# GpSimd subtracts the softmax maxima of all sixteen attention units of a block, not of eight

## The chip, the core and the metric

One core of one Trainium2 chip. The metric is the device time of one execution in microseconds; the time before is the median of three executions. The profile comes from one more execution.

## What is computed

A decoder layer over 64 sequences of 128 tokens with 128 features: self-attention with 16 heads and relative positions, cross-attention, a mixture of experts, each followed by a layer norm. The change touches the first part alone:

```python
scores = jnp.einsum('bhqd,bhkd->bhqk', q, k) / scale
scores = scores + (c2p + p2c) / scale            # relative positions
probs = jax.nn.softmax(scores, axis=-1)
ctx = jnp.einsum('bhqk,bhkd->bhqd', probs, v)
out = ctx @ Wo + bo + hidden_states
mu = jnp.mean(out, axis=-1, keepdims=True)
var = jnp.mean(jnp.square(out - mu), axis=-1, keepdims=True)
out = (out - mu) * jax.lax.rsqrt(var + LN_EPS) * ln_scale + ln_bias
x = _layernorm(x + out)
```

## The kernel before

The attention stage works on 16 blocks of four sequences. A block has sixteen **units**; a unit `u` is one sequence and four heads, so four score matrices of 128 x 128. Each engine has its own program, a loop over the steps `u` of a block, and the order of an engine's work is the order in which this code is written. Semaphores tie the engines together.

What happens to one unit: TensorE writes the scores to a PSUM bank (L448, L451; two banks). VectorE adds the second position term and takes the row minimum (the scores are negated), which leaves `T` and `nm` in SBUF (L709, four times a main instruction and a read of the accumulator; it raises `t_ok`). ScalarE makes `E`, the exponential. TensorE transposes `E` two steps later (L459), ScalarE copies the transposed tile to `ET` three steps later (L601), and TensorE multiplies by the values (L485) four steps later. `T` and `E` have three buffers each, chosen by `u % 3`.

The exponential has two forms. In units of `EARLY_MAX`, 6 to 13, GpSimd first subtracts the minimum in place (L369, `take_max`, which waits for `t_ok` and raises `p_ok`), and ScalarE runs one instruction of 128 x 512 (L610). In the other units, 0 to 5, 14 and 15, GpSimd isn't asked; ScalarE runs four of 128 x 128, each with its head's minimum as its bias (L613).

Between these steps stands other work. Steps 0 to 2: the next block's inputs are transposed and projected (TensorE L402, L407, L408, L412; ScalarE L574 and L582; VectorE L676 and L683). From step 6 on, 16 bucket tiles of the next block, two in a step: TensorE L425, ScalarE L588 (`HM`), VectorE L693. After step 15 come the next block's position chunks (TensorE L440, copied out by ScalarE L596 and VectorE L702), while the last units are finished; here ScalarE's L620 copies the sums of four units to `OC`, and that frees the bank for the next L485.

The two layer norms of the block before are spread over the steps of this one by `NORM_STEPS`: on VectorE statistics at step 2 (L731), variances at 3 (L738, L741), `centred` at 4 (L751), `first_norm` at 5 (L759), the second norm's statistics and variances at 6 and 7 (L731, L738, L741), its end at 9 (L766). The inverse roots are powers on GpSimd (L365, `power`): it waits for VectorE's L741, and L759 and L766 wait for it.

GpSimd does its work of a block in this order: `copy_block` (L299, `XB` for the next block), the first power, units 6 and 7, the second power, units 8 to 13, `residuals` (L304 twice), `spread_keys` (L313, then L315 four times, which makes `KD` for the next block's scores), `values_out` (L323).

Of the kernel before, what the change touches and what calls it, by code (L numbers as in the profile page):

```python
# [39 lines left out]
NORM_STEPS = (2, 3, 4, 5, 6, 7, 9)  # L40
# [1 line left out]
CONSTS, TAB, BUILT = 21, 10, 4  # L42
DVE_CHUNKS = tuple((c, 1) for c in range(1, CHUNKS))
ACT_CHUNKS = tuple((c, f) for c in range(CHUNKS) for f in range(2) if (c, f) not in DVE_CHUNKS)
EARLY_MAX = range(6, 14)
VCOLS = 32
HALVES = ((0, 0), (0, 1), (1, 0))

# [94 lines left out]
def attention_stage(nc, held, dr, X):  # L143

    with ExitStack() as ctx:
# [6 lines left out]
        def sem(name):  # L152
            return held.enter_context(nc.semaphore("a_" + name))
# [74 lines left out]
        t_ok = Count(sem("t_ok"), UNITS, credit=2)  # L228
        p_ok = Count(sem("p_ok"), len(EARLY_MAX))
        e_ok = Count(sem("e_ok"), UNITS, credit=3)  # L230
# [63 lines left out]
        def _(pool):  # L294
            def copy_block(i, nxt):
                if nxt:
                    hold(pool, spare_pool, xT_ps.sem, xT_ps.at(i, 1))
                at = (i + 1) * NB if nxt else 0
                pool.tensor_copy(XB[:, :, :], X[:, bass.ds(at, NB), :]).then_inc(xb.sem, 1)  # L299

            def residuals(i):
                hold(pool, spare_pool, link_s.sem, link_s.at(i, 0))
                for vec, dst in ((bo_all, XO), (bias_all, XL)):
                    pool.tensor_tensor(dst[:, :, :], X[:, bass.ds(i * NB, NB), :],  # L304
                                       vec[:, :].rearrange("p (a h) -> p a h", a=1).to_broadcast([P, NB, H]),
                                       ALU.add).then_inc(x_ok.sem, 1)

            def spread_keys(i, nxt):
                if nxt:
                    hold(pool, spare_pool, s_ps.sem, s_ps.at(i, UNITS))  # L310
                hold(pool, spare_pool, qn_in.sem, qn_in.at(i, qn_in.per * (1 + nxt)))
                hold(pool, spare_pool, kn_in.sem, kn_in.at(i, kn_in.per * (1 + nxt)))
                pool.tensor_copy(QS[:, :, :, :], QN[:, :, :, :].rearrange("p g s b -> p g b s"))  # L313
                for h in range(HG):
                    last = pool.tensor_scalar(KD[:, :, h, :, :], KN[:, :, :, :].rearrange("p g s b -> p g b s"),  # L315
                                              group_mask[:, h:h + 1], 1.0, ALU.mult, ALU.mult)
                last.then_inc(kd_ok.sem, 1)

            def values_out(i, nxt):
                if nxt:  # L320
                    hold(pool, spare_pool, pv.sem, pv.at(i, UNITS))
                hold(pool, spare_pool, vn_ok.sem, vn_ok.at(i, 1 + nxt))
                pool.tensor_copy(V[:, :, :, 0:DH], VN[:, :, :, :]).then_inc(v_ok.sem, 1)  # L323
# [39 lines left out]
            def power(i, n):  # L363
                pool.wait_ge(var_ok.sem, var_ok.at(i, n + 1))
                pool.tensor_tensor(rstd[:, :], rstd[:, :], half[:, :], ALU.pow).then_inc(rstd_ok.sem, 1)  # L365

            def take_max(i, u):
                hold(pool, spare_pool, t_ok.sem, t_ok.at(i, u + 1))
                pool.tensor_tensor(T[:, u % 3, :, :], T[:, u % 3, :, :],  # L369
                                   nm[:, u % 3, :].rearrange("p (h a) -> p h a", a=1).to_broadcast([P, HG, S]),  # L370
                                   ALU.subtract).then_inc(p_ok.sem, 1)

            def body(i, first=False, last=False):
                if not last:
                    copy_block(i, 1)
                if not first:
                    power(i - 1, 0)
                for u in range(UNITS):
                    if u in EARLY_MAX:
                        take_max(i, u)  # L380
                    if u == NORM_STEPS[5] and not first:
                        power(i - 1, 1)
                residuals(i)
                if not last:
                    spread_keys(i, 1)
                    values_out(i, 1)

            body(0, first=True)
            with pool.Fori(1, NBLK - 1) as i:
                body(i)  # L390
            body(NBLK - 1, last=True)
            for n in range(2):
                power(NBLK - 1, n)
# [177 lines left out]
        def _(act):  # L571
# [31 lines left out]
            def exponentials(i, u):  # L603
                if u in EARLY_MAX:
                    act.wait_ge(p_ok.sem, p_ok.at(i, EARLY_MAX.index(u) + 1))
                else:
                    act.wait_ge(t_ok.sem, t_ok.at(i, u + 1))
                act.wait_ge(et_ps.sem, et_ps.at(i, u - 2))
                if u in EARLY_MAX:
                    act.activation(E[:, u % 3, :, :], T[:, u % 3, :, :], ACT.Exp, scale=-1.0).then_inc(e_ok.sem, 1)  # L610
                    return
                for h in range(HG):
                    last = act.activation(E[:, u % 3, h, :], T[:, u % 3, h, :], ACT.Exp, bias=nm[:, u % 3, h:h + 1],  # L613
                                          scale=-1.0)
                last.then_inc(e_ok.sem, 1)
# [1535 lines left out]
```

## Time and profile before

| what | value |
|---|---|
| three executions | 2919.28, 2921.62, 2922.58 us; median 2921.62 us |
| the profiled execution | 2919.2 us; its span in the profile is 2917.4 us |
| busy over the span | PE 2411.7, DVE 2223.2, ACT 2293.1, POOL 711.4 us |
| blocks' loop of the attention stage | about 73 to 1030 us |

Times within the span are counted from its start. PE is TensorE, DVE VectorE, ACT ScalarE, POOL GpSimd. In a timeline a row gives the start, the length and the instruction; "x4" is four instructions in a row, and brackets say how long the engine stood idle before and who released it. In a group by line the number before the bar is the sum and the mean length in ns (the lengths overlap, since an engine starts the next instruction before the last one has ended); behind the bar stands the idle time before these instructions.

### The profile page before, as it was taken

The page shows a single profiled execution, that of the slowest core. Times are in us where ns is not written, and L with a number is a line of the kernel's source. Part 1 is how long each engine was busy: PE and PEld are TensorE (multiplying, and loading weights), DVE is VectorE, ACT ScalarE, POOL GpSimd, SP SyncE. Part 2 cuts the span into 40 slices and gives each one's busy share as a digit, 9 for nine tenths or more (in the row PEclk, how much of TensorE's full clock was granted, in tenths as well). Part 3 has the DMA queues.
Part 4 walks back from the last instruction along what each step waited for, and adds up shares of the span by engine and source line. Part 5 has one row for each costly group of instructions (what it writes and reads, how often), then busy time and mean ns, then how long its engine had stood idle before and what let it go on. Part 6 is the DMA issues. An engine that isn't in the chain of part 4 may idle for free. (4 is left out here: it accounts for less than half of the span.)

```text
span 2917.4 us, 64307 instructions
## 1 busy us (share of the span) xinstructions
PE 2411.7 (83%) x18180; PEld 1323.8 (45%) x18199; DVE 2223.2 (76%) x6591; ACT 2293.1 (79%) x4255; POOL 711.4 (24%) x565
## 2 busy tenths in 40 slices
PE   2777777777777724865779999999999999999997
PEld 1555555555555413642434444444444444444443
DVE  3677777777777667777558888888888888888887
ACT  1777777777777635333679999999999999999996
POOL 3334353344334400122411111111111111111114
PEclk7899999999999956988789999999999999999999
DMA  3000000000000010000011121121111211111113
GB/s 76 13 17 17 11 11 12 20 11 11 11 17 15 1 42 1 0 29 0 0 36 53 43 58 43 44 58 43 53 49 43 58 43 45 56 43 56 45 43 87
DMA packets 182540, 96.04 MB, mean 33 GB/s; under 512 B 22539, under 2 KB 179291, under 8 KB 182491
## 3 DMA queue, kind: packets, MB, share of 16 engines
q1 hardware_dynamic: 182491, 95.45, 11.7%
q8 instruction: 23, 0.38, 0.1%
q14 instruction: 26, 0.21, 0.0%
HBM read 78.10 MB, written 4.73 MB: 28 GB/s over the span
## 5 line engine op out<-in xcount | busy, mean ns | idle before, releaser
L1971 DVE TENSOR_TENSOR c_Hl<-c_HF,c_Hh 128x512 f16<-128x512 f32 x1028 | 679.6, 688 | 161.2 <-ACT c_Hh L1858 144.9
L1854 ACT ACTIVATE c_HF<-c_H,c_b 128x512 f32<-128x512 f32 x1028 | 710.6, 691 | 64.4 <-PE c_H L1793 44.4
L1858 ACT ACTIVATE c_Hh<-c_H,c_b 128x512 f16<-128x512 f32 x1028 | 706.1, 687 | 0.0
L1909 POOL TENSOR_TENSOR c_EX<-c_euler,c_D 128x16 f32<-128x16 f32 x65 | 188.6, 2902 | 1195.2 <-DVE c_D L1944 1195.2
L1791 PE MATMUL c_H<-c_Ch,SH 128*128 128x512 f16 x1028 | 390.7, 380 | 0.0
L1792 PE MATMUL c_H<-c_Cl,SH 128*128 128x512 f16 x1028 | 390.6, 380 | 0.0
L1793 PE MATMUL c_H<-c_Ch,SH 128*128 128x512 f16 x1028 | 390.5, 380 | 0.0
L1802 PE MATMUL c_Y<-c_Hh,SH 128*128 128x512 f16 x1024 | 388.1, 379 | 0.1
L1804 PE MATMUL c_Y<-c_Hl,SH 128*128 128x512 f16 x1024 | 388.1, 379 | 0.0
L1803 PE MATMUL c_Y<-c_Hh,SH 128*128 128x512 f16 x1024 | 388.1, 379 | 0.0
L709 DVE CUSTOM_DVE_ANT_0 a_T<-a_S,a_POS 128x128 f32<-128x128 f32 x1024 | 234.9, 285 | 70.0 <-PE a_S L451 63.1
L459 PE MATMUL a_E<-a_ident,a_E 128*128 128x128 f32 x1024 | 159.5, 279 | 67.5 <-ACT a_ET L601 66.8
L693 DVE TENSOR_TENSOR a_AB<-a_G,a_HM 128x512 f16<-128x512 f32 x256 | 164.4, 683 | 65.2 <-ACT a_HM L588 61.6
L588 ACT ACTIVATE a_HM<-a_G,a_low_rows 128x512 f16<-128x512 f32 x256 | 161.9, 686 | 63.1 <-PE a_G L425 63.1
L369 POOL TENSOR_TENSOR a_T<-a_T,a_nm 128x512 f32<-128x512 f32 x128 | 133.3, 1041 | 300.2 <-DVE a_nm L709 300.2
L613 ACT ACTIVATE a_E<-a_T,a_nm 128x128 f32<-128x128 f32 x512 | 162.8, 390 | 54.5 <-DVE a_nm L709 53.0
L1979 DVE SCALAR_TENSOR_TENSOR c_PR<-c_Y,c_b,c_CWB 128x512 f32<-128x512 f32 x256 | 191.1, 747 | 2.4 <-DMA c_CWB<-c_rows 1.5
L485 PE MATMUL a_O<-a_ET,a_V 128*32 128x128 f32 x2048 | 110.4, 288 | 66.6 <-ACT a_OC L620 66.6
L451 PE MATMUL a_S<-a_ident,a_POS 128*128 128x128 f32 x1024 | 160.8, 280 | 0.0
L1793 PEld LDWEIGHTS c_H<-c_Ch,SH 128*128 128x128 f16 x1028 | 100.7, 98 | 122.2 <-issue 1.4
L1802 PEld LDWEIGHTS c_Y<-c_Hh,SH 128*128 128x128 f16 x1024 | 100.1, 98 | 121.8 <-issue 0.6
L1804 PEld LDWEIGHTS c_Y<-c_Hl,SH 128*128 128x128 f16 x1024 | 100.2, 98 | 120.8
(296 smaller groups left out, 4382.7 us busy)
## 6 DMA issues: line engine op xcount, KB each, us to landing
c_CWB<-c_rows SPq DMA_DIRECT2D x260, 256.0 KB, 4.1
a_QN<-a_QH SPq DMA_DIRECT2D x128, 32.0 KB, 1.8
a_KN<-a_KH SPq DMA_DIRECT2D x128, 32.0 KB, 1.8
out<-d_O SPq DMA_DIRECT2D x16, 256.0 KB, 2.3
a_QN<-a_QL SPq DMA_DIRECT2D x64, 32.0 KB, 1.9
a_KN<-a_KL SPq DMA_DIRECT2D x64, 32.0 KB, 1.8
CUR<-in_ctx SPq DMA_DIRECT2D x1, 1848.0 KB
c_rows<-c_CWR SPq DMA_DIRECT2D x65, 8.0 KB, 1.4
```

What stands on the lines that cost most here:

```text
L709: last = dve.tensor_tensor_reduce(out=T[:, u % 3, h, :], in0=bS[u % 2][:, h * S:(h + 1) * S], in1=POS[:, h // 2, row_x(1, g, h % 2, b), :] ...
L1791: pe.matmul(dst, W1h[:, e, cols], Ch[:, j, :], start=True, stop=False)
L1792: pe.matmul(dst, W1h[:, e, cols], Cl[:, j, :], start=False, stop=False)
L1793: pe.matmul(dst, W1l[:, e, cols], Ch[:, j, :], start=False, stop=True).then_inc(h_ps.sem, 1)
L1802: pe.matmul(dst, W2h[:, e, f, :], Hh[:, g % 2, f, :], start=f == 0, stop=False)
L1803: pe.matmul(dst, W2l[:, e, f, :], Hh[:, g % 2, f, :], start=False, stop=False)
L1804: last = pe.matmul(dst, W2h[:, e, f, :], Hl[:, g % 2, f, :], start=False, stop=f == OC - 1)
L1854: act.activation(HF[:, k % 4, :], bH[k % 4][:, :], ACT.Gelu_apprx_tanh, bias=b1[:, g % EXPERTS, f:f + 1], scale=1.0 / WSCALE).then_inc(hf_ ...
L1858: act.activation(Hh[:, g % 2, f, :], bH[k % 4][:, :], ACT.Gelu_apprx_tanh, bias=b1[:, g % EXPERTS, f:f + 1], scale=1.0 / WSCALE).then_inc( ...
L1909: pool.tensor_tensor(EX[:, :, :].rearrange("p t e -> p (t e)"), euler[:, :], D[:, :, :].rearrange("p t e -> p (t e)"), ALU.pow).then_inc(e ...
L1971: dve.tensor_tensor(Hl[:, g % 2, f, :], HF[:, k % 4, :], Hh[:, g % 2, f, :], ALU.subtract)\
L1979: dve.scalar_tensor_tensor(PR[:, g % 2, :], bY[g % 2][:, :], b2[:, e:e + 1], CWB[:, m, e, :], ALU.add, ALU.mult).then_inc(p_ok.sem, 1)
```

## The change

`EARLY_MAX` covers all sixteen units, so `take_max` is called sixteen times in a block, and ScalarE takes the one-instruction form everywhere. The first power moves from ahead of the units to behind the subtraction of unit 3 (`NORM_STEPS[1]`); the second stays where it was, behind that of unit 7 (`NORM_STEPS[5]`).

```diff
-EARLY_MAX = range(6, 14)
+EARLY_MAX = range(0, 16)
...
                 if not last:
                     copy_block(i, 1)
-                if not first:
-                    power(i - 1, 0)
                 for u in range(UNITS):
                     if u in EARLY_MAX:
                         take_max(i, u)
-                    if u == NORM_STEPS[5] and not first:
-                        power(i - 1, 1)
+                    if u in (NORM_STEPS[1], NORM_STEPS[5]) and not first:
+                        power(i - 1, (NORM_STEPS[1], NORM_STEPS[5]).index(u))
                 residuals(i)
```

GpSimd's program of the last block, where the rows stand unrolled (`a_rstd` is written by a power, `a_T` by `take_max`, `a_XO` and `a_XL` by `residuals`):

```order
-L365 TENSOR_TENSOR a_rstd<-a_rstd,a_half 128x4
-L369 TENSOR_TENSOR a_T<-a_T,a_nm 128x512 x2
-L365 TENSOR_TENSOR a_rstd<-a_rstd,a_half 128x4
-L369 TENSOR_TENSOR a_T<-a_T,a_nm 128x512 x6
...
+L369 TENSOR_TENSOR a_T<-a_T,a_nm 128x512 x4
+L365 TENSOR_TENSOR a_rstd<-a_rstd,a_half 128x4
+L369 TENSOR_TENSOR a_T<-a_T,a_nm 128x512 x4
+L365 TENSOR_TENSOR a_rstd<-a_rstd,a_half 128x4
+L369 TENSOR_TENSOR a_T<-a_T,a_nm 128x512 x8
 L304 TENSOR_TENSOR a_XO<-X,a_bo_all 128x512
 L304 TENSOR_TENSOR a_XL<-X,a_bias_all 128x512
```

Six subtractions now stand ahead of unit 6's, four of them ahead of the first power, and two more stand ahead of the residuals, which in the other blocks have `spread_keys` behind them.

ScalarE's program at steps 3 to 6 of a block, before the change:

```order
L601 ACTIVATE a_ET<-a_E 128x512
L613 ACTIVATE a_E<-a_T,a_nm 128x128 x4
L601 ACTIVATE a_ET<-a_E 128x512
L613 ACTIVATE a_E<-a_T,a_nm 128x128 x4
L601 ACTIVATE a_ET<-a_E 128x512
L588 ACTIVATE a_HM<-a_G,a_low_rows 128x512 x2
L610 ACTIVATE a_E<-a_T 128x512
```

The same steps after the change (two lines shorter, so 601 is 599, 610 is 608 and 588 is 586):

```order
L599 ACTIVATE a_ET<-a_E 128x512
L608 ACTIVATE a_E<-a_T 128x512
L599 ACTIVATE a_ET<-a_E 128x512
L608 ACTIVATE a_E<-a_T 128x512
L599 ACTIVATE a_ET<-a_E 128x512
L586 ACTIVATE a_HM<-a_G,a_low_rows 128x512 x2
L608 ACTIVATE a_E<-a_T 128x512
```

The order is the same; four narrow instructions have become one wide one, and the exponential still stands ahead of the copy `ET` and the tiles `HM`.

## Rows read from the trace of the kernel before

**Rows 1.** Group by line, attention stage: the narrow exponentials.

```profile
L613 ACT ACTIVATE a_E<-a_T,a_nm 128x128 f32<-128x128 f32 x512 | 162.8, 390 | 54.5 <-DVE a_nm L709 53.0
```

**Rows 2.** Stretches of one block: length, then each engine's busy time, TensorE's clock.

```profile
510.16:518.56 8.40, 7.35 (x71) 5.23 (x69) 8.18 (x54) 7.01 (x20) 1.53 (x2) 1.00 0.19 51
562.00:564.00 2.00, 2.00 (x11) 1.74 (x10) 0.93 (x8) 0.63 (x1) 0.00 (x0) 0.50 0.00 0
```

**Rows 3.** Timeline of ScalarE, units 3 to 7 of that block.

```profile
512.49 1.28 ACT L613 ACTIVATE a_E<-a_T,a_nm 128x128 f32<-128x128 f32 x4 [1.28 <-DVE a_nm L709]
...
516.00 1.28 ACT L613 ACTIVATE a_E<-a_T,a_nm 128x128 f32<-128x128 f32 x4
...
517.67 1.25 ACT L588 ACTIVATE a_HM<-a_G,a_low_rows 128x512 f16<-128x512 f32 x2
...
521.93 0.63 ACT L610 ACTIVATE a_E<-a_T 128x512 f32<-128x512 f32 x1 [0.54 <-POOL a_T L369]
522.47 0.58 ACT L620 ACTIVATE a_OC<-a_O 128x512 f32<-128x512 f32 x1
```

**Rows 4.** Timeline of VectorE, units 3 to 7 of that block, some rows.

```profile
512.78 0.17 DVE L741 TENSOR_SCALAR a_rstd<-a_mv 128x4 f32<-128x4 f32 x1
...
513.99 1.13 DVE L751 SCALAR_TENSOR_TENSOR a_R<-a_R,a_mv,a_scale_all 128x128 f32<-128x128 f32 x4
...
515.89 1.14 DVE L759 SCALAR_TENSOR_TENSOR a_R<-a_R,a_rstd,a_XL 128x128 f32<-128x128 f32 x4
...
518.56 1.27 DVE L693 TENSOR_TENSOR a_AB<-a_G,a_HM 128x512 f16<-128x512 f32 x2
...
520.59 0.09 DVE L709 DVE_READ_ACCUMULATOR2_ANT a_nm<- 128x1 f32 x1
...
521.00 0.92 DVE L741 TENSOR_SCALAR a_rstd<-a_mv 128x4 f32<-128x4 f32 x1
```

**Rows 5.** Timeline of GpSimd, unit 7.

```profile
520.86 1.04 POOL L369 TENSOR_TENSOR a_T<-a_T,a_nm 128x512 f32<-128x512 f32 x1 [1.77 <-DVE a_nm L709]
```

**Rows 6.** All instructions of three lines: shortest, median and longest in ns.

```profile
L741 DVE TENSOR_SCALAR a_rstd<-a_mv x32: 170/172/922, 157.1 to 1026.4; 128x4 f32<-128x4 f32 x32
...
L2084 DVE SCALAR_TENSOR_TENSOR d_nb<-d_mv,d_rstd x16: 147/150/547, 2883.3 to 2912.6; 128x4 f32<-128x4 f32 x16
...
L1321 POOL COPY b_r<-SH x64: 392/399/994, 1149.3 to 1269.9; 77x256 f32 x64
```

**Rows 7.** Timelines, VectorE beside GpSimd: the output stage, then the last block.

```profile
2887.88 0.55 DVE L2084 SCALAR_TENSOR_TENSOR d_nb<-d_mv,d_rstd 128x4 f32<-128x4 f32 x1 [1.06 <-POOL d_rstd L2051]
...
2887.80 0.61 POOL L2043 COPY d_CB<-CUR 128x512 f32 x1
...
1022.46 1.13 DVE L751 SCALAR_TENSOR_TENSOR a_R<-a_R,a_mv,a_scale_all 128x128 f32<-128x128 f32 x4
...
1022.63 1.05 POOL L365 TENSOR_TENSOR a_rstd<-a_rstd,a_half 128x4 f32<-128x4 f32 x1 [13.47 <-DVE a_rstd L741]
```

**Rows 8.** Timelines at the block's unit 15: ScalarE, then VectorE.

```profile
545.22 1.28 ACT L613 ACTIVATE a_E<-a_T,a_nm 128x128 f32<-128x128 f32 x4 [0.87 <-DVE a_nm L709]
546.41 0.57 ACT L620 ACTIVATE a_OC<-a_O 128x512 f32<-128x512 f32 x1
...
548.08 0.69 DVE L702 COPY a_POS<-a_S 128x512 f32<-128x512 f32 x1 [2.89 <-PE a_S L440]
```

**Rows 9.** Timelines, GpSimd's ends of three blocks, and the next block's first scores.

```profile
482.20 1.27 POOL L304 TENSOR_TENSOR a_XO<-X,a_bo_all 128x512 f32<-128x512 f32 x1
...
540.72 1.28 POOL L304 TENSOR_TENSOR a_XO<-X,a_bo_all 128x512 f32<-128x512 f32 x1
...
546.40 8.51 POOL L315 TENSOR_SCALAR a_KD<-a_KN,a_group_mask 128x2048 f16<-128x2048 f16 x4
...
601.11 1.27 POOL L304 TENSOR_TENSOR a_XO<-X,a_bo_all 128x512 f32<-128x512 f32 x1
...
561.15 0.47 PE L448 MATMUL a_S<-a_KD,a_QS 96*128 96x512 f16 x1 [1.12 <-DVE a_POS L702]
```

## The prediction

> **What bounds the kernel now.** I read the busy shares first: TensorE, VectorE and ScalarE are all between 76 and 83%, GpSimd is at 24%, so no single engine is full. The attention stage is then a matter of who waits for whom, step by step, and the views that count are the timelines of one block.
>
> In the groups by line, look at what ended the idle time ahead of the narrow exponentials: 53.0 of 54.5 us ended with VectorE's L709, and their instructions are 162.8 us of busy time [rows 1]. A narrow exponential starts as soon as VectorE has released it in about half of the units. For those units the latency from L709 to `E` counts, and not how long ScalarE is busy.
>
> From the copy of the values at 510.16 to the first `HM` tile's use at 518.56, VectorE is busy 8.18 of 8.40 us [rows 2]. It is the bound of steps 3 to 5, where the first layer norm is squeezed in, while ScalarE has 1.4 us to spare. At unit 5 ScalarE starts at 516.00, 0.11 us behind the start of L759, which itself follows unit 5's L709 on VectorE [rows 3, 4]. So ScalarE keeps pace with VectorE there and hasn't a queue to work off. The next thing, two `HM` tiles at 517.67, stands on ScalarE behind unit 5's exponential and one `ET` copy; VectorE's L693 at 518.56 needs the first of them, and had about 0.2 us to spare (half of 1.25 us after 517.67 is 518.3) [rows 3, 4].
>
> At the end of a block the chain is plainer: unit 15's exponential at 545.22 waited 0.87 us for VectorE; `OC` follows at 546.41; it frees the bank for the product L485, behind which the position chunks stand on TensorE, and VectorE, with nothing to do, waits 2.89 us until the first chunk reaches it at 548.08 [rows 8].
>
> **The change, part by part.**
>
> *The hop through GpSimd.* Unit 7 shows it: the last accumulator read ends at 520.68, the subtraction runs from 520.86 to 521.90, the wide exponential starts at 521.93 [rows 3 to 5]. That is 1.25 us after L709, against some 0.05 us for a narrow one: 1.2 us more.
>
> *The exponential.* From the start of a narrow one to the next instruction pass 1.19 us (545.22 to 546.41), from the start of a wide one 0.54 us (521.93 to 522.47) [rows 3, 8]. It gives back 0.65 us, eight times a block. Where ScalarE was waiting for VectorE, what stands behind the exponential is therefore 1.2 - 0.65 = 0.55 us later. The gain could only count where ScalarE was late already, in unit 1 for instance; but there the projections on TensorE and then VectorE set the pace, so I cost it at nothing.
>
> *Collision with L741.* The variance add L741 takes 170 to 172 ns in half of its 32 cases and up to 922 ns [rows 6]. The long one of the block read here, at 521.00, lies in unit 7, right behind L709: the subtraction of unit 7 runs until 521.90 and L741 ends at 521.92 [rows 4, 5]. The one in unit 3, at 512.78, is short, since GpSimd has nothing to do there [rows 4]. After the change unit 3 looks like unit 7: the subtraction is asked for at the same distance from L709, so this L741 takes 0.92 us too. That is 0.75 us on VectorE, in the stretch where VectorE is the bound, in 15 blocks.
>
> *Collision with `centred` and `first_norm`.* L751 and L759 (1.13 and 1.14 us for four) read two tensors from SBUF [rows 4]. No row of before has one of them beside a subtraction, so the price is bounded. Below: beside a power L751 kept its 1.13 us (1022.46, power at 1022.63), so nothing [rows 7]; but the power reads four elements a partition and the subtraction 512. Above: L2084, also with two tensors in SBUF, takes 150 ns and once 547; there a GpSimd copy of 512 elements ran from 2887.80 to 2888.41, and L2084 ended at 2888.43 [rows 6, 7]. So it was held until the copy had ended. The subtraction is nearer to this copy, and I take a full hold. Who loses? GpSimd's copy L1321, 399 ns as a rule, took 994 ns once, so GpSimd can be the one who is held [rows 6]. In the block, with VectorE 0.75 us late, `centred` runs from 514.74 to 515.87 and the subtraction of unit 4 is asked for at 515.0: it waits 0.87 us and runs to 516.91. `first_norm` wants to start at 516.64. If it goes first at 516.91, the subtraction of unit 5 runs from 518.05 to 519.09, the exponential starts at 519.12, an `ET` copy follows at 519.66 and `HM` at 520.14, 2.5 us later than 517.67. If the subtraction of unit 5 goes first, to 517.95, `first_norm` and all of VectorE behind it are 2.1 us late instead. Less the 0.2 us that L693 had to spare: L693 is 1.9 to 2.3 us late, and I take 2.1. Without these two holds it would be 0.75 + 0.55 - 0.2 = 1.1 us. The Trainium skill, SBUF — State Buffer, section "Who interferes with whom", says that a VectorE instruction with two SBUF inputs contends with a GpSimd instruction that reads SBUF, and that the one that comes second is blocked wholly. By that rule the block loses the 2.1 us, and L2084's row agrees; L751 beside the power doesn't show such a block.
>
> From unit 6 on all three engines and GpSimd are late by about the same, and their program isn't changed, so nothing there gives it back. The second L741 and L766 already stand beside a subtraction.
>
> *Units 14 and 15.* The exponential of 14 has slack before TensorE uses it. Unit 15's delay goes to `OC`, the product, the chunks and VectorE's 2.89 us wait: 0.55 us [rows 8].
>
> *GpSimd's end of the block.* The residuals started at 540.72, before unit 15 was done; now they start when its subtraction ends, 545.2 + 0.18 + 1.04 = 546.4 [rows 8, 9]. Two residuals (2.5 us), L313 (2.0) and L315 (8.51) bring `KD` to 559.4; the next scores, which need it, started at 561.15 and will start 0.55 us later [rows 9]. Margin 2.3 us, so this costs nothing; `XB`, 1.2 us behind `KD`, is wanted 0.65 us behind the start of the scores and has 1.7 us. The transfers of queries and keys wait for older `KD`, and don't move.
>
> *The sum.* 15 blocks with a norm (2.1 + 0.55) = 39.8 us; block 0, without a norm, 0.9 us (0.55 at its end, some 0.3 ahead of the tiles). Together 40.7 us on the profiled execution's 2919.2: 2959.9 us. That execution was 2.4 us below the median of 2921.62, so the forecast is **2962 us**.
>
> **The rivals.**
>
> *Only L741 collides* (L751 and L759 pass untouched, as beside the power): 15 x (1.1 + 0.55) + 0.9 = 25.7 us, 2947 us. For it: L751's row. Against it: L2084's.
>
> *Faster: the hop is hidden.* `T` and `E` have three buffers, so the hop may vanish and ScalarE's saving count. 65 of the 128 narrow exponentials weren't waiting for VectorE (it ended the idle time in 63 cases); they would give 65 x 0.65 = 42 us at most, the 63 others cost 63 x 0.55 = 35: 7 us faster, 2915 us. It decides only if ScalarE had a queue to work off in steps 3 to 5. Against it: ScalarE had 1.4 us free there and VectorE 0.2 [rows 2], and the collisions come on top.
>
> *GpSimd's chain becomes the bound.* If `KD` needs 3 us more than worked out, each of 15 blocks loses 0.7 us more: 2973 us. It decides from 2.3 us on. Against it: L315's durations hardly vary.
>
> *The clock.* Some blocks take longer: from 482.20 to 540.72 are 58.52 us, to 601.11 are 60.39 [rows 9]. In the second TensorE stood idle around 561 and the granted clock fell to 0.50, its lower level, from 562 to 564 [rows 2]. Six of 14 such intervals are long. A shifted rhythm can give this to more blocks or fewer: 8 x 1.9 = 15 us more (2977) or 11 us less (2951). Longer idle times speak for more.
>
> *No change:* the delays would have to be swallowed by VectorE's waits in units 8 to 13; nothing there is early while the rest is late.
>
> **How the numbers follow.** Two full holds 50%, only L741 20%, more through clock or GpSimd 15%, hidden hop and faster 8%, within 0.2% (about what a measurement of this kernel tells from no change, 6 us) 7%. The range runs from the L741 case less a few clock dips, 2943, to the two holds with all dips and a late `KD`, 2986. Faster 0.08, same 0.07, slower 0.85.
>
> **What would show it.** The L741 of unit 3 at 0.92 us in 15 blocks; L751 or L759 lengthened, or some subtractions of 1.9 us; the exponential of unit 15 1.2 us behind L709, VectorE's wait for the first chunk at 3.4 us; `KD` ready before the next scores, which still wait for VectorE; about 61 us for a block that took 58.5. I am wrong if blocks stay at 58.5 us, if L741 of unit 3 stays at 0.17 us, or if the scores at a block's start wait for GpSimd.

## The result, and the profile after

The changed kernel takes 2966.16 us (median of four executions, 2959.89 to 2970.15) against 2921.85 us for the kernel before: a ratio of 1.0148, 95% interval 1.0134 to 1.0162. It is 44 us slower. The profiled execution has a span of 2968.4 us and a mean granted clock of 0.933; the one of before had 2917.4 us and 0.941.

In the changed kernel's code the lines behind the change stand two lower: L741, L751, L759, L693, L709 are now L739, L749, L757, L691, L707, and the only exponential left is L608.

First the timeline of VectorE in the changed kernel, steps 2 to 6 of one middle block (start, length, instruction):

```profile
474.98 0.69 DVE L681 TENSOR_TENSOR a_VN<-a_M,a_bv_all 128x512 f32<-128x512 f32 x1 [0.59 <-PE a_M L410]
...
477.61 0.92 DVE L739 TENSOR_SCALAR a_rstd<-a_mv 128x4 f32<-128x4 f32 x1
479.28 1.92 DVE L749 SCALAR_TENSOR_TENSOR a_R<-a_R,a_mv,a_scale_all 128x128 f32<-128x128 f32 x4
481.96 1.97 DVE L757 SCALAR_TENSOR_TENSOR a_R<-a_R,a_rstd,a_XL 128x128 f32<-128x128 f32 x4
484.70 0.86 DVE L729 BATCH_NORM_STATS2 a_st<-a_R 128x6 f32<-128x128 f32 x4
485.48 1.27 DVE L691 TENSOR_TENSOR a_AB<-a_G,a_HM 128x512 f16<-128x512 f32 x2
```

And GpSimd beside it, the subtractions of units 3, 4 and 5 with the first power between:

```profile
477.46 1.04 POOL L369 TENSOR_TENSOR a_T<-a_T,a_nm 128x512 f32<-128x512 f32 x1 [1.85 <-DVE a_nm L707]
478.60 1.02 POOL L365 TENSOR_TENSOR a_rstd<-a_rstd,a_half 128x4 f32<-128x4 f32 x1
479.60 1.19 POOL L369 TENSOR_TENSOR a_T<-a_T,a_nm 128x512 f32<-128x512 f32 x1
482.22 1.04 POOL L369 TENSOR_TENSOR a_T<-a_T,a_nm 128x512 f32<-128x512 f32 x1 [1.43 <-DVE a_nm L707]
```

All three VectorE steps of the first norm have grown: the variance add from 0.17 to 0.92 us, `centred` from 1.13 to 1.92, `first_norm` from 1.14 to 1.97 [rows 4]. Together that is 2.37 us. The subtraction of unit 4 started 0.32 us behind `centred` and took 1.19 us where the others take 1.04: it lost 0.15 us and then held VectorE. `first_norm` was overtaken 0.26 us after its start, and there the subtraction lost nothing (1.04 us). L691 follows the statistics at once: VectorE, and nothing else, is late there. The moved power ends at 479.62, and `first_norm`, which needs it, follows VectorE's L707 at 481.96 without a wait. The stretch from the copy of the values to the first tile was 8.40 us long (510.16 to 518.56) and is 10.50 us now (474.98 to 485.48).

All instructions of these lines: shortest, median, longest in ns. With 32 variance adds a median of 919 says that more than half are long, as against 172 before [rows 6]; of the 64 instructions of each norm step only one in four is held, and then for some 0.8 us.

```profile
L739 DVE TENSOR_SCALAR a_rstd<-a_mv x32: 170/919/921, 162.6 to 1076.9; 128x4 f32<-128x4 f32 x32
...
L749 DVE SCALAR_TENSOR_TENSOR a_R<-a_R,a_mv,a_scale_all x64: 335/341/1127, 164.3 to 1073.7; 128x128 f32<-128x128 f32 x64
...
L757 DVE SCALAR_TENSOR_TENSOR a_R<-a_R,a_rstd,a_XL x64: 339/342/1184, 167.0 to 1075.0; 128x128 f32<-128x128 f32 x64
```

At unit 15, timelines of ScalarE and, a block earlier, of VectorE and GpSimd:

```profile
514.07 0.63 ACT L608 ACTIVATE a_E<-a_T 128x512 f32<-128x512 f32 x1 [2.25 <-POOL a_T L369]
514.61 0.58 ACT L618 ACTIVATE a_OC<-a_O 128x512 f32<-128x512 f32 x1
...
454.38 0.69 DVE L700 COPY a_POS<-a_S 128x512 f32<-128x512 f32 x1 [3.46 <-PE a_S L438]
...
452.10 1.26 POOL L304 TENSOR_TENSOR a_XO<-X,a_bo_all 128x512 f32<-128x512 f32 x1
...
456.55 8.51 POOL L315 TENSOR_SCALAR a_KD<-a_KN,a_group_mask 128x2048 f16<-128x2048 f16 x4
...
467.46 0.39 PE L446 MATMUL a_S<-a_KD,a_QS 96*128 96x512 f16 x1 [1.12 <-DVE a_POS L700]
```

VectorE's wait for the first chunk has gone from 2.89 to 3.46 us [rows 8]. `KD` is ready at 465.06, 2.4 us before the next block's first scores at 467.46, which wait for VectorE as before [rows 9].

To see where a block's time goes I cut it at three points of VectorE's timeline, each from start to start: **head**, from the copy of the values to the first tile (L693); **middle**, from there to the first copy of a position chunk out of bank S (L702); **tail**, from there to the next block's copy of the values. Among the 14 intervals of each kernel these values recur to 0.01 us in the shortest ones (six intervals before, two after):

```
               head   middle   tail    sum
before         8.42   29.51    20.60   58.53
after         10.50   30.07    20.60   61.17
difference     2.08    0.56     0       2.64
```

The head is 10.50 in thirteen of the fourteen intervals after, and 8.42 (or 8.40, 8.41) in twelve before. The one of the fourteen that isn't longer, 8.52 in both kernels, is that of block 0, which has no norm. Middle and tail are longer in some blocks of either kernel, and there the granted clock is lower; in five intervals of the changed kernel a middle of 30.7 us or more is followed by a tail of 20.41. The stretches below are of the changed kernel (length; busy time of TensorE, of its weight load, of VectorE, ScalarE and GpSimd; the clock; the DMA share and rate): a block and a bit with 0.84, and within it 18 us at the lower level, 0.50; the interval ahead of the head shown above, from 413.30, had 0.97.

```profile
413.30:475.00 61.70, 46.71 (x590) 31.63 (x589) 46.63 (x202) 41.15 (x76) 32.82 (x28) 0.97 0.05 13
327.00:345.00 18.00, 15.97 (x271) 12.04 (x268) 11.57 (x27) 10.44 (x21) 10.49 (x8) 0.50 0.00 0
284.00:350.00 66.00, 52.39 (x590) 35.78 (x591) 47.30 (x205) 41.63 (x76) 32.72 (x27) 0.84 0.04 12
```

The 14 intervals sum to 831.6 us before and 874.5 after, 42.9 more. Thirteen of them have a norm in the head and one, block 0's, has none: 13 x 2.64 + 0.56 = 34.9. The other 8 us stand in intervals whose clock is lower, 4.7 of them in block 0's (60.0 us before at a clock of 0.97, 65.3 after at 0.84). The profiled spans differ by 51 us: 37.0 in the 14 blocks with a norm and tiles, 0.6 for the hop in block 0, 8 of slower clock, 4.7 in the last block, and 0.7 ahead of the first interval and behind the attention stage.

### The profile page after: what moved, and what is told of

It reads as the page before. It is cut to its first block and busy times, and to the rows that moved or that the text cites. A ratio compares the mean times of both kernels' runs of the same rounds, so it can differ in the third digit from the quotient of the medians.

```text
span 2968.4 us, 64207 instructions
## 1 busy us (share of the span) xinstructions
PE 2441.2 (82%) x18180; PEld 1336.7 (45%) x18199; DVE 2259.3 (76%) x6591; ACT 2211.8 (75%) x3871; POOL 844.6 (28%) x693
## 5 line engine op out<-in xcount | busy, mean ns | idle before, releaser
L369 POOL TENSOR_TENSOR a_T<-a_T,a_nm 128x512 f32<-128x512 f32 x256 | 268.3, 1048 | 476.6 <-DVE a_nm L707 476.1
L608 ACT ACTIVATE a_E<-a_T 128x512 f32<-128x512 f32 x256 | 161.4, 630 | 229.3 <-POOL a_T L369 228.4
L707 DVE CUSTOM_DVE_ANT_0 a_T<-a_S,a_POS 128x128 f32<-128x128 f32 x1024 | 234.5, 284 | 68.3 <-PE a_S L449 59.3
L457 PE MATMUL a_E<-a_ident,a_E 128*128 128x128 f32 x1024 | 166.6, 288 | 87.8 <-ACT a_ET L599 86.3
L691 DVE TENSOR_TENSOR a_AB<-a_G,a_HM 128x512 f16<-128x512 f32 x256 | 164.3, 683 | 63.6 <-ACT a_HM L586 58.9
L457 PEld LDWEIGHTS a_E<-a_ident,a_E 128*128 128x128 f32 x1024 | 120.7, 147 | 109.6 <-ACT a_E L608 93.1
```

What stands on the lines that cost most here:

```text
L369: pool.tensor_tensor(T[:, u % 3, :, :], T[:, u % 3, :, :], nm[:, u % 3, :].rearrange("p (h a) -> p h a", a=1).to_broadcast([P, HG, S]), AL ...
L457: last = pe.transpose(bE[slot_of(w) % 2][:, h * S:(h + 1) * S], E[:, w % 3, h, :], ident[:, :])
L707: last = dve.tensor_tensor_reduce(out=T[:, u % 3, h, :], in0=bS[u % 2][:, h * S:(h + 1) * S], in1=POS[:, h // 2, row_x(1, g, h % 2, b), :] ...
```

## The experiments

Each kernel is compared with the kernel before on the same chip; the line numbers of the rows are those of each kernel. All that differ in `EARLY_MAX` alone keep the power in its new place.

**Units 14 and 15 alone.**

```diff
-EARLY_MAX = range(0, 16)
+EARLY_MAX = range(6, 16)
```

> GpSimd subtracts in units 6 to 15 (8 to 13 of before, and the two last), units 0 to 5 keep four narrow exponentials. My theory has two separate places per block: the hop in unit 15 costs 0.55 us in each of 16 blocks and the rest of the loss lies in units 3 to 5. It expects about 9 us over the kernel before (some 2931 us), the wait of VectorE for the first chunk at 3.4 to 3.5 us and the variance add of step 3 at 0.17 us. A rival, that GpSimd's late end of the block (keys for the next one) costs as well, expects more, 15 to 25 us, with the first scores waiting for GpSimd.

2932.48 us against 2921.55, ratio 1.0045 (1.0028 to 1.0062). The wait has its 3.46 us, here in VectorE's timeline:

```profile
496.65 0.69 DVE L700 COPY a_POS<-a_S 128x512 f32<-128x512 f32 x1 [3.46 <-PE a_S L438]
```

Head 8.42, middle 30.08, tail 20.60. Eleven microseconds of 44, where 9 were expected. The rival of a late `KD` falls: the shortest blocks lose 0.57 us and nothing in the tail, and the next block's first scores still wait for VectorE (L700, 1.12 us).

**Units 0 to 5 alone.**

```diff
-EARLY_MAX = range(0, 16)
+EARLY_MAX = range(0, 14)
```

> GpSimd subtracts in units 0 to 13, units 14 and 15 keep four narrow exponentials. My theory expects 2.1 us in each of the 15 blocks with a norm, about 32 us over before (some 2954 us), with the variance add of step 3 at 0.92 us and both four-instruction norm steps at about 1.95 us. If the two places weren't additive, this run and the one with units 14 and 15 alone would not add up to the 44 us of the whole change.

2955.41 us, ratio 1.0113 (1.0096 to 1.0130): 34 us. Head 10.50, middle 29.49 where undisturbed. 11 + 34 is 45, so the two places add up to the whole change (44).

**Units 0, 1, 2.**

```diff
-EARLY_MAX = range(0, 16)
+EARLY_MAX = (0, 1, 2) + tuple(range(6, 14))
```

> GpSimd subtracts in units 0, 1, 2 and 6 to 13. There the hop is present but no VectorE instruction of the kinds that were held stands behind it. If the loss in the first half comes from the holds, this is within 3 us of before. If the hop through GpSimd itself costs 0.55 us each time that ScalarE waited for VectorE (unit 2 did), it is up to 8 us slower.

2921.79 us, ratio 0.9998 (0.9988 to 1.0007); head 8.42. The hop is there in three more units and costs nothing, and neither does the power's new place.

**Unit 3.**

```diff
-EARLY_MAX = range(0, 16)
+EARLY_MAX = (3,) + tuple(range(6, 14))
```

> GpSimd subtracts in unit 3 and 6 to 13. Only the variance add L741 of step 3 can be held: 0.75 us in 15 blocks, 11 us over before (2933 us). If a hold on VectorE there were absorbed, it is as before; if the hop were what costs, it adds 0.55 us a block to it, about 19 us.

2934.55 us, ratio 1.0046 (1.0029 to 1.0062): 13 us. The variance add is held here too, and the two norm steps aren't (longest instruction 347 and 351 ns). But the 0.75 us of the hold become 0.48 in the head, 8.89 to 8.90 us, and in five blocks the head is 10.04, so that the 11 us expected were nearly met by luck. The timeline of VectorE in such a block, and the two stretches, long and short:

```profile
456.23 0.93 DVE L739 TENSOR_SCALAR a_rstd<-a_mv 128x4 f32<-128x4 f32 x1
...
463.64 1.29 DVE L691 TENSOR_TENSOR a_AB<-a_G,a_HM 128x512 f16<-128x512 f32 x2 [0.56 <-ACT a_HM L586]
...
453.60:463.64 10.04, 8.40 (x69) 5.88 (x68) 9.05 (x54) 6.38 (x17) 3.10 (x3) 0.83 0.19 52
635.01:643.90 8.89, 7.25 (x71) 5.23 (x69) 8.86 (x54) 6.38 (x17) 2.58 (x3) 1.00 0.19 52
```

With the clock at 0.83 in this stretch instead of 1.00, L691 waits for ScalarE's tile. The clock stood at 0.50 from 459 to 462, behind a wait of TensorE of 1.64 us that the short heads have as well, so why it fell in these five is open. In all 14 intervals of the kernel before the head stayed within 8.40 to 8.59. Fifteen heads at 0.48 us more are 7.2 us and the five long ones add 5 x 1.15 = 5.8, together the 13.

**Units 4 and 5.**

```diff
-EARLY_MAX = range(0, 16)
+EARLY_MAX = (4, 5) + tuple(range(6, 14))
```

> GpSimd subtracts in units 4, 5 and 6 to 13; unit 3 keeps its narrow exponentials. Only the two norm steps with two SBUF inputs can be held, 0.79 and 0.83 us by the changed kernel's profile. The head run lost 2.08 us in its shortest blocks and the unit-3 run 0.48, so 1.6 us a block, 24 us over before (about 2945 us), with both steps at about 1.95 us for four and the variance add of step 3 at 0.17. If the holds only occur because unit 3's hold has shifted VectorE against GpSimd, both steps stay at 1.13 us and the run is as before.

2952.99 us, ratio 1.0106 (1.0088 to 1.0124): 31 us, 7 more than expected. The head is 10.11, that is 1.70 us more, close to the 1.6 that I expected; but no block has both middle and tail at their shortest, with a mean clock of 0.934 over the run. So both norm steps are held without unit 3's help: their longest instructions take 1197 and 1183 ns where the kernel before has 351 and 352, 1.68 us together. All subtractions take 1.04 us here, so that GpSimd loses nothing. That is VectorE's timeline of a block, the variance add short and `centred` long:

```profile
465.21 0.17 DVE L739 TENSOR_SCALAR a_rstd<-a_mv 128x4 f32<-128x4 f32 x1
...
466.42 1.99 DVE L749 SCALAR_TENSOR_TENSOR a_R<-a_R,a_mv,a_scale_all 128x128 f32<-128x128 f32 x4
```

**Steps that read one tensor from SBUF.** In both kernels `centred` and `first_norm` become statistics of the same rows; what they compute is left out.

```diff
-                    last = dve.scalar_tensor_tensor(R[:, b, :], R[:, b, :], mv[:, b, 0:1], scale_all[:, :],
-                                                    ALU.subtract, ALU.mult)
+                    last = dve.bn_stats(st[:, b, :], R[:, b, :])
...
-                    last = dve.scalar_tensor_tensor(R[:, b, :], R[:, b, :], rstd[:, b:b + 1], XL[:, b, :],
-                                                    ALU.mult, ALU.add)
+                    last = dve.bn_stats(st[:, b, :], R[:, b, :])
```

> The kernel before with both norm steps (centred and first_norm) replaced by statistics of the same rows, which read one SBUF tensor; it leaves out the centring and the first normalisation. Four statistics take 0.87 us, four of the steps 1.13, so up to 0.5 us a block less: 2913 to 2922 us. It is the base for the next one.

> The changed kernel with the same two steps replaced by statistics (centring and first normalisation left out). If a second SBUF input is what exposes a VectorE instruction to GpSimd's subtraction, the statistics keep 0.87 us and this is only 16 to 26 us slower than its base (variance add and the hop of unit 15). If the loss in units 4 and 5 is the hop through GpSimd or any VectorE instruction is held, it is 40 to 45 us slower than its base, as in the unaltered pair.

2920.63 us for the first (ratio to the kernel before 0.9993, 0.9975 to 1.0010) and 2955.23 for the second (1.0111, 1.0093 to 1.0129). On the first question the trace of the second is plain. In its list of instructions the statistics beside the subtractions take what they take elsewhere:

```profile
L749 DVE BATCH_NORM_STATS2 a_st<-a_R x64: 269/272/287, 164.0 to 1060.9; 128x6 f32<-128x128 f32 x64
```

Of the 128 statistics in the place of the two steps 105 overlap a subtraction, so these steps aren't held, and the rival that any VectorE instruction is held falls. That the second SBUF tensor is what exposes the norm steps isn't shown by it alone: the statistics also write 6 columns instead of 128, and the variance add, which is held, reads one tensor. The time is 35 us above its base, where I had expected 16 to 26. The head went from 8.09 to 9.10 us, the middle from 29.53 to 30.10, so 1.58 us in the shortest block, 24 us in 15; the rest goes with a slower clock (mean 0.929; 13 of the 14 intervals are longer than the shortest). And 1.0 us in the head is more than one held variance add: L691 waits 0.50 us for ScalarE's tile there.

**The variance add as another instruction.** The eps stands as a third column beside mean and variance, and a reduction over two columns gives the same sum. First in the kernel before:

```diff
-        mv = sb("mv", [P, NB, 2])
+        mv = sb("mv", [P, 2, NB, 3])
...
-                dve.tensor_scalar(rstd[:, :], mv[:, :, 1], (1e-7, 1e-5)[k], None, ALU.add).then_inc(var_ok.sem, 1)
+                dve.tensor_reduce(rstd[:, :], mv[:, k, :, 1:3], AX_X, ALU.add).then_inc(var_ok.sem, 1)
```

> The kernel before with the variance add made as a tensor_reduce over the variance and a constant beside it, the same sum. If the kind of instruction decides, none of its 32 cases lasts 0.92 us any more, where 15 did. If VectorE is the bound in step 7, that gives 0.75 us in 15 blocks, 11 us (2911 us); if the wait for the tiles behind it takes it up, the time is within 3 us of before. If every instruction with an SBUF input were held, the 0.92 us stay.

2923.41 us, ratio 1.0005 (0.9995 to 1.0015). All 32 take 160 to 165 ns in its trace, 15 of them beside a subtraction, and the shortest blocks keep 58.53 us. The kind of instruction decides, and in step 7 of the kernel before the hold of 0.75 us cost nothing. Then in the changed kernel:

> The changed kernel with the variance add as a tensor_reduce, the same sum. No variance add is held any more. With the two norm steps still held, I expect what unit 3 alone cost to come back: 0.5 to 0.75 us in 15 blocks, 8 to 11 us less than the changed kernel's 2966, so 2955 to 2958. If the subtraction of unit 3 then only meets the next VectorE instructions and costs the same there, it stays at 2966.

2958.24 us, 8 us less than the changed kernel (ratio to the kernel before 1.0125, 1.0108 to 1.0142, as against 1.0148). Timeline of VectorE:

```profile
465.87 0.16 DVE L741 TENSOR_REDUCE a_rstd<-a_mv 128x4 f32<-128x8 f32 x1
467.08 1.92 DVE L751 SCALAR_TENSOR_TENSOR a_R<-a_R,a_mv,a_scale_all 128x128 f32<-128x128 f32 x4
```

The head is 10.04 instead of 10.50, so removing unit 3's hold gives back 0.46 us, as much as adding it alone had cost (0.48).

**Unit 14.**

```diff
-EARLY_MAX = range(0, 16)
+EARLY_MAX = range(6, 15)
```

> GpSimd subtracts in units 6 to 14. My theory says that the exponential of unit 14 has slack before TensorE uses it, and that unit 15 alone costs the 0.58 us of the tail: the time is that of before within 3 us and the wait of VectorE for the first chunk stays at 2.89 us. If both units share the loss, it is about 5 us slower and the wait about 3.2 us.

2922.10 us, ratio 0.9995 (0.9984 to 1.0005); the wait is 2.89 us again:

```profile
494.67 0.69 DVE L700 COPY a_POS<-a_S 128x512 f32<-128x512 f32 x1 [2.89 <-PE a_S L438]
```

The loss at the end of a block is unit 15's alone.

**All units where nothing was to pay.**

```diff
-EARLY_MAX = range(0, 16)
+EARLY_MAX = (0, 1, 2) + tuple(range(6, 15))
```

> GpSimd subtracts in units 0, 1, 2 and 6 to 14: all those where I found nothing to pay. ScalarE is relieved of 4 x 0.65 us a block. If ScalarE's saving were worth anything where it is free, this would be faster than before; my theory says no change, within 3 us.

2922.81 us, ratio 1.0008 (0.9998 to 1.0019). Relieving ScalarE of 2.6 us a block in these four units is worth nothing. No experiment pointed to a version faster than the kernel before.

**Nothing that can be held.** The changed kernel with the reduction and with both norm steps replaced by statistics.

> The changed kernel without any VectorE instruction that can be held in steps 3 to 5: the variance add as a reduce, the two norm steps replaced by statistics (centring and first normalisation left out). What is left against its base (the kernel before with the same replacement, shortest blocks 58.22 us) is the hop: 0.57 us at unit 15 and, if the hop also reaches the tiles behind unit 5, 0.55 us there, so shortest blocks of 59.3 us and 17 us more in all. If the hop is hidden in steps 3 to 5, blocks of 58.8 us and 9 us more.

2963.81 us (2952.50 to 2970.10), ratio to the kernel before 1.0146 (1.0115 to 1.0177). This expectation failed: I had said 17 us above the base of 2920.63, and it is 43. The head is 8.96; the shortest middle is 30.10 and the undisturbed tail 20.59, though no block has both: 59.65 together, 1.43 us above the base's 58.22, of which 0.87 in the head, where I had allowed 0.55. That is 21 us in 15 blocks. The other half goes with the clock: the profiled execution's mean of 0.924 is the lowest of all the profiled ones, and the four executions of this kernel go from 2952.50 us at 0.928 to 2970.10 us at 0.917. Stretches of its trace, two middles that should be 30.1 us long and one head:

```profile
408.70:440.80 32.10, 23.46 (x222) 15.05 (x221) 20.61 (x101) 21.72 (x41) 13.24 (x14) 0.92 0.03 8
471.00:502.00 31.00, 22.31 (x206) 14.36 (x204) 19.82 (x100) 20.62 (x39) 12.80 (x13) 0.92 0.03 7
399.70:408.70 9.00, 7.31 (x69) 5.03 (x68) 7.83 (x54) 5.27 (x10) 5.70 (x6) 1.00 0.19 52
```

In the head nothing is held any more, and its last part shows what bounds it: ScalarE's tiles wait for TensorE's L425, behind the exponentials that came late.

```profile
405.29 0.63 ACT L610 ACTIVATE a_E<-a_T 128x512 f32<-128x512 f32 x1 [0.87 <-POOL a_T L371]
...
407.89 1.27 ACT L588 ACTIVATE a_HM<-a_G,a_low_rows 128x512 f16<-128x512 f32 x2 [0.24 <-PE a_G L425]
...
408.70 1.29 DVE L693 TENSOR_TENSOR a_AB<-a_G,a_HM 128x512 f16<-128x512 f32 x2 [0.35 <-ACT a_HM L588]
```

So the hop does cost in the head when it is alone, and VectorE waits for ScalarE there. It isn't added to the holds. In the changed kernel ScalarE begins its two tiles at 484.30, so that the first is done at about 484.9, and VectorE comes to it at 485.48:

```profile
484.30 1.26 ACT L586 ACTIVATE a_HM<-a_G,a_low_rows 128x512 f16<-128x512 f32 x2
```

Of two delays on parallel ways the longer counts. The 0.87 us are measured against a head that the replacement had shortened to 8.09 us; against the 8.42 of the kernel before they are 0.54, so they can't be carried over to the norm steps as they were.

## Why the prediction was right

*The size and the sign.* 2962 us forecast, 2966 measured, within the range; the likeliest case came. A block was to lose 2.1 + 0.55 us and loses 2.08 + 0.56 in the shortest ones. That the 2.1 came out to 0.02 us is luck in part, as the third paragraph shows.

*"Collision with L741": the hold was right, its price wasn't.* It is held in all 15 blocks for 0.75 us as forecast. Alone it moved the head by 0.48. The timelines show where the rest went: before, VectorE's next instruction started 0.19 us behind the end of L741 (512.95 to 513.14), and now it starts 0.09 us ahead of that end (478.44, 478.53). That takes up 0.28 of the 0.75 us. The two rows, of the kernel before and of the changed one:

```profile
513.14 0.29 DVE L709 CUSTOM_DVE_ANT_0 a_T<-a_S,a_POS 128x128 f32<-128x128 f32 x1 [0.19 <-issue]
```

```profile
478.44 0.28 DVE L707 CUSTOM_DVE_ANT_0 a_T<-a_S,a_POS 128x128 f32<-128x128 f32 x1
```

*"Collision with `centred` and `first_norm`": the hold was right, and who loses was wrong.* I had the subtraction of unit 4 wait 0.87 us for all of `centred`. It waited 0.15 us, for one instruction, and went between the four; then VectorE was held, 0.79 us, and 0.83 in `first_norm`. The row I leaned on, L1321, was a copy held by instructions of another kind (`tensor_scalar` of 128x512, L1334), and four times and not once. The sum came out right by another way: I had the tiles late on ScalarE, or VectorE late by a subtraction that had itself been late. What came was VectorE's three holds, 2.37 us less the 0.28 above. My lower bound of 1.9 us was also wrong in itself, since it took ScalarE's 0.2 us to spare off a delay of VectorE, which had none. The rival that only L741 collides falls with L749's 1.92 us and with the run of units 4 and 5.

The page's rule (the Trainium skill, SBUF — State Buffer, "Who interferes with whom") agrees with the two norm steps (two SBUF tensors, held beside subtractions) and with the statistics and the reduction (one, 272 and 161 ns, not held). The variance add reads one tensor and was held all the same, 0.92 us for 0.17; the sentence that I drew on doesn't cover it, and its hold is shown by these runs alone. The power is against the rule as I put it: it reads SBUF as well, and four L751 beside it kept 1.13 us [rows 7]. The section says, of VectorE's modes that take the pair of ports shared with GpSimd, that who issues first gets the pair for the whole instruction; the trace adds that "instruction" is meant singly: the other engine got in between four in a row.

*"The hop through GpSimd": right at unit 15* (0.56 us, and unit 14 free), and free at units 0 to 2. In steps 3 to 5 I had summed it with the hold of L741 to 1.1 us for the case without the two others; with statistics in their place this measured 1.01. Alone it is 0.87 against the shortened head, and beside all three holds nothing: they make up the head's 2.08 us by themselves.

*GpSimd's end of the block: right.* Margin 2.3 us forecast, 2.4 seen.

*"From unit 6 on nothing gives it back": right* for what enters late, since the head's loss appears whole in the sum. But the reduction in the kernel before showed that step 7's own hold is free; the delay has slack there, and the argument would not have told me.

*The rival "faster" falls:* relieving ScalarE in four units a block changed nothing.

*The clock: a term of its own.* I had left it out of the sum and put it into the range. It cost about 8 us more than before in the 14 intervals. More than half of that is the first block: it lost 4.85 us between the starts of its `xT` copies where I had put 0.9, from 60.71 us before to 65.56 us, in a stretch whose clock was 0.95 before and 0.84 after. The last block, without tiles and projections, lost 4.7 us instead of 2.65 (GpSimd's residuals, 50.04 apart before and 54.75 after), and there too the clock was lower. The stretch of the kernel before, then two of the changed one:

```profile
956.62:1006.66 50.04, 36.83 (x556) 25.81 (x556) 33.77 (x184) 34.36 (x81) 23.81 (x19) 1.00 0.00 1
```

```profile
1007.45:1062.20 54.75, 39.27 (x555) 27.61 (x556) 35.34 (x182) 29.63 (x57) 32.19 (x28) 0.94 0.00 1
1045.50:1049.50 4.00, 3.69 (x22) 2.71 (x22) 0.99 (x9) 1.44 (x4) 1.04 (x1) 0.57 0.01 2
```

How much of the last block's 2 us more is the clock, and how much waiting for exponentials, no run separates. The profiled spans differ by 51 us and the medians by 44, so a single execution can carry some microseconds more of this than the median does. At an undisturbed clock the losses of the blocks sum to about 40 us, by an estimate: 14 x 2.64, 0.56 in the first block and some 2.65 in the last. The forecast had 40.7, so the 4 us by which it fell short of the medians are left to the clock, for which its sum had no term.

*What stays open:* why a block falls into a slower clock, and so why the runs with statistics in place of the norm steps, whose undisturbed sections add up to nearly the same (59.65 us with the reduction, 59.80 without), differ by 9 us in their medians. Nor did I try the norm steps with one SBUF tensor and their computation kept.

## What to carry to other kernels

An engine with three quarters of its time free isn't free of cost: before work moves to GpSimd, list the VectorE instructions that will run beside it. Here the `scalar_tensor_tensor` steps with two SBUF tensors and the `tensor_scalar` with one lost 0.75 to 0.85 us each beside a subtraction of 1.04 us, and `bn_stats` and `tensor_reduce` lost nothing. A saving on ScalarE counts only where ScalarE is late; the row to look at is what ended its idle time.

Cut a repeated block at two or three fixed instructions and compare the shortest sections of two traces. They agree to 0.01 us where the clock is undisturbed, and so separate a mechanism of half a microsecond from the clock, which the medians mix.

## What the runs showed of the hardware that I had not expected

In all 15 blocks the subtraction that came while VectorE had four instructions with two SBUF inputs in a row waited for one of them only (1.19 instead of 1.04 us) and then held the next for 0.8 us. The same sum made with `tensor_scalar` takes 0.17 us alone and 0.92 beside a subtraction, and with `tensor_reduce` 0.16 in either case.

When the clock fell in a head of the unit-3 run, the head took 10.04 us at 0.83 instead of 8.89 at 1.00, since then TensorE and ScalarE, and no longer VectorE, set the pace. No head of the kernel before had a lower clock, so what such a fall costs without the delay isn't shown.
